# A block of ripple attention and mixture of experts: adding DMAs merge weighted terms that TensorE summed alone, and identity turns stand ahead of three more of its waits

## The chip, the cores and the metric

The kernel runs on one core of a Trainium2 chip. The metric is the time of one execution on the device in microseconds (us); the time before is the median of three runs. A core has TensorE (PE in the profile; its weight loads are PEld), VectorE (DVE), ScalarE (ACT), GpSimd (POOL) and SyncE (SP), each with its own queue of instructions that it works off in order, and 16 DMA engines that carry the transfers of all queues. Engines wait for each other by semaphores. TensorE's granted clock is given as a share of 2.4 GHz: 1.00 or, at the lower level of 1.2 GHz, 0.50.

## What is computed

The input x has four batches of 1024 tokens with 128 channels, in float32. The block is x + LN(attention(LN(x))), called x2, and then x2 + LN(experts(LN(x2))). The attention is a sum of three parts:

```
offsets = 0, 1, 2, 4, ..., 512                      # 11 earlier positions of each token
tele = softmax(q . k[pos - offsets] / 4) weighs v[pos - offsets]     # 8 heads of 16 channels
conv = 7 taps along the tokens, per channel, of v
low  = elu features of q and k: fq (fk^T v) / (fq . sum fk)
attention = x + (tele + conv + low) @ Wo
```

The feed-forward part sends each token to two of eight experts by a sigmoid gate, each a hidden layer of 64 with GELU, and adds a shared expert. All of it must come out; the change touches how the 11 weighted terms of `tele` and the term `low` are added up, and in what order that happens.

## The kernel before

The four batches run through a pipeline. In iteration b of the main loop (b = 0 to 4) the attention of batch b runs beside the experts of batch b - 1, which are cut into two halves of 512 tokens, called units: u0 = 2b - 2 and u1 = 2b - 1. Also beside it run the layer norm and the projections of batch b + 1. There is no planner: the order on each engine is written out by hand in five program blocks (SyncE, POOL, ScalarE, VectorE, TensorE), and each waits on semaphores with the counts that the other blocks raise.

A batch has eight tiles of 128 tokens. In the stage that the change touches, VectorE weighs the values of tile j (`weigh`, L929 to L950; its instructions are L940): three multiplications write up to 11 terms of 128 x 128 into one of four buffers in SBUF (TERM_BUFS = 4), first those with whole-tile offsets, then the offset 128, then in one instruction the seven shifted ones (1 to 64), 128 x 896 elements. Between them it works off steps of the gates of u1, for tiles 0 to 3 and only where there are experts to do (b > 0). TensorE then sums the terms of the tile (`sum_terms`, L1252 to L1265): a turn against the identity for the low-rank term (L1260) and one for each live term (L1263), all accumulated in one PSUM bank, so that the sum arrives turned. Tiles 0 to 3 fill the bank as the first half of the batch, tiles 4 to 7 as the second. When a half is there, VectorE adds the convolution to it (`add_conv`, L967 to L972), which frees the bank, and TensorE takes the output product (`output`, L1267 to L1275):

```
live = [m for m in range(NV) if TERMS[m] < P or TERMS[m] // P <= j]
for m in live:
    ins = pe.matmul(dst, terms[:, j % TERM_BUFS, m, :], ident[:], is_transpose=True,
                    start=False, stop=(m == live[-1]))
```

The order of the terms in a buffer is 128, 512, 256, 0, 1, 2, 4, 8, 16, 32, 64. Tile 0 has 8 live terms, tile 4 and those behind it 11.

Around these sums TensorE's queue also holds the experts: the sum over the experts of u0 (`experts_out`, L1358) in front of tile 0, the projections of q and v of batch b + 1 (`project`, L1183) in front of tiles 1 and 5, hidden layers of u1 (L1322) in front of tile 2, the turn of the gates of u1 (L1332) in front of tile 4 and its spread gates (`spread_gates`, L1344) in front of tiles 5 and 6. VectorE needs the spread gates for `gate_hidden` (L1063), which stands in its queue behind tiles 5 and 7. In front of all this come, for u1, the turn of x3 (`turn_x3`, L1284), the gate logits (`gate_logits`, L1295), and the turned logits (`turn_logits`, L1301); for u0 they come earlier in the iteration, between the sums of the scores (L1231).

POOL's queue in an iteration holds the 1/sqrt steps of the layer norms (`rstd_of`, L433 and L435), the tap sums of the convolution as DMAs that add (`add_tap`, L453 and L454, 512 KB each), and for the experts the scale of u0's outputs (`ln4`, L489), and the addition of the residual (`add_residual`, L497 to L502, line L501), which waits for ScalarE's `scale_outputs` (L700). The part that matters is, in this order: the last tap sums, `ln4(u0)`, `add_residual(u0)`, `ln2(2b)`, then the first tap sums of the next batch. SyncE's queue stores the outputs of u0 when `add_residual` is done, and behind that loads the x of batch b + 2 (L338).

`keep_busy(n, bank)` (L1363 to L1367) runs n turns of the identity into a PSUM bank, whose results nobody reads; before the change it stands at the kernel's start, ahead of the last score sums (12 turns) and at three places in the tail.

Of the kernel before, what the change touches and what calls it, by code (L numbers as in the profile page):

```python
# [20 lines left out]
P = 128  # L21
# [27 lines left out]
WARM_UP = 28  # L49
FILL_SUM = 12  # L50
FILL_FRONT = 5
CH = 5


N_DMA = 16
SHIFT_ROWS = 112
N_SHIFT_DMA = 16 * sum(3 if P - off > SHIFT_ROWS else 2 for off in SHIFTS)
N_PSA_FULL, N_PSA_FREE = 16, 14
# [14 lines left out]
LAST_BANKS = (0, 1, 2, 3, 0, 1, 2, 0)  # L73

LAST_GATE_STEPS = (12, 15, 18, 21)


def upto(b, per_batch, n):
# [37 lines left out]
def block_kernel(nc, x, Wqkv, Wo, conv_w, gate_W, W1, b1, W2, b2, Ws1, bs1, Ws2, bs2, route_scale, out):  # L116
# [4 lines left out]
    with ExitStack() as ctx:  # L121
# [6 lines left out]
        def sem(name):  # L128
            return ctx.enter_context(nc.semaphore(name))
# [109 lines left out]
        logit_ready, prob_ready, softmax_step = sem("logit_ready"), sem("prob_ready"), sem("softmax_step")  # L239
        v_shifted, low_ready, low_used = sem("v_shifted"), sem("low_ready"), sem("low_used")  # L240
        terms_ready, terms_summed = sem("terms_ready"), sem("terms_summed")
        tap_scaled, sums_added, side_added = sem("tap_scaled"), sem("sums_added"), sem("side_added")
        conv_step = sem("conv_step")
        hT_ready, y_ready = sem("hT_ready"), sem("y_ready")
# [134 lines left out]
        def _(pool):  # L379
# [64 lines left out]
            def ln1(b):  # L444
# [5 lines left out]
                pool.wait_ge(ln1_step, upto(b - 1, 2, 2))  # L450
                nc.gpsimd.tensor_tensor(nmr1[:], neg_mean[:, b % 3, :], rstd1[:], ALU.mult).then_inc(ln1_ready, 1)

            def add_tap(b, into, tap, added):  # L453
                nc.gpsimd.dma_start(tap_home(b, into), tap_home(b, tap), accum_op=ALU.add).then_inc(added, N_DMA)  # L454

# [51 lines left out]
            for b in range(B + 1):  # L507
                attn, ffn, more = b < B, b >= 1, b < B - 1
                u0, u1 = 2 * b - 2, 2 * b - 1
                if ffn:  # L510
                    ln2(u1)
                if 2 <= b < B:
                    ln4(u0 - 1)
                if attn and b:
                    sum_taps_second(b)
                if more:
                    ln1(b + 1)
                if ffn and attn:
                    ln3(u1)
                if attn and b:  # L520
                    sum_taps_third(b)
                if ffn and attn:
                    ln4(u0)
                    add_residual(u0)
                if attn:
                    ln2(2 * b)
                if more:
                    sum_taps_first(b + 1)
                if attn:
                    ln3(2 * b)  # L530
                if not attn:
                    ln3(u1)
                    ln4(u0 - 1)
                    ln4(u0)
                    ln4(u1)
# [265 lines left out]
        def _(dve):  # L801
# [278 lines left out]
            for b in range(B + 1):  # L1080
# [29 lines left out]
                if attn:  # L1110
# [14 lines left out]
                    for j in range(NT):  # L1125
                        def two_gate_steps(n):

                            if ffn and j < TPH:
                                gates(u1, range(2 * (3 * j + n), 2 * (3 * j + n + 1)))

                        weigh(b, j, two_gate_steps)
                        if ffn:
                            if j in (5, 7):
                                gate_hidden(u1, range(j - 5, j - 3))
                        if j == TPH:
                            add_conv(b, 0)
                    residual(2 * b)
                    add_conv(b, 1)
                    if more:
# [16 lines left out]
        def _(pe):  # L1156
# [95 lines left out]
            def sum_terms(b, j):  # L1252

                pe.wait_ge(terms_ready, upto(b, NT, j + 1))
                if j == 0:
                    pe.wait_ge(low_used, b + 1)
                elif j == TPH:
                    pe.wait_ge(hT_ready, upto(b, 2, 1))
                dst = psH[:, bass.ts(j % TPH, P)]
                pe.matmul(dst, low_terms[:, j, :], ident[:], is_transpose=True, start=True, stop=False)  # L1260
                live = [m for m in range(NV) if TERMS[m] < P or TERMS[m] // P <= j]
                for m in live:
                    ins = pe.matmul(dst, terms[:, j % TERM_BUFS, m, :], ident[:], is_transpose=True,  # L1263
                                    start=False, stop=(m == live[-1]))
                ins.then_inc(terms_summed, 1)  # L1265
# [18 lines left out]
            def turn_x3(u):  # L1284

                if u == 2 * B - 1:
                    pe.wait_ge(front_free, upto(u, N_FRONT, 0))
                elif u:
                    pe.wait_ge(hidden_free, upto(u, N_HIDDEN, -1))
                pe.wait_ge(xn3_ready, u + 1)  # L1290
                for n, j in enumerate(unit_tiles(u)):
                    ins = pe.transpose(front(u, X3)[:, bass.ts(n, P)], xn3[:, j, :], ident[:])
                ins.then_inc(front_full, 1)

            def gate_logits(u):  # L1295
                if 0 < u < 2 * B - 1:
                    pe.wait_ge(hidden_free, upto(u, N_HIDDEN, 0))
                pe.wait_ge(front_free, upto(u, N_FRONT, 1))
                pe.matmul(front(u, C4), w1[:, 4 * P:5 * P], x3T[:, half_cols(u)], start=True, stop=True).then_inc(front_full, 1)

            def turn_logits(u):  # L1301
                pe.wait_ge(front_free, upto(u, N_FRONT, 2))
                for n, j in enumerate(unit_tiles(u)):
                    ins = pe.transpose(front(u, LOGITS)[:, bass.ts(n, EXPERTS)], gate_shared[0:EXPERTS, bass.ts(j, P)],
# [193 lines left out]
```

## Time and profile before

| what | us |
|---|---|
| median of three runs (302.92 to 304.26) | 303.39 |
| the profiled execution, its own time | 304.41 |
| its span in the profile | 302.7 |
| TensorE busy in the span | 248.6 (82%) |
| VectorE busy | 240.0 (79%) |
| ScalarE busy | 192.6 (64%) |
| POOL busy | 84.4 (28%) |

The rows below come from the one profiled execution. Times of day in it are us from the start of its span; some 1.7 us of its own time lie outside the span. A busy share is a mean over stages that have different limits, so it doesn't say which engine a stage waits for. That is read from the timeline: an instruction's row ends, in brackets, with the idle time of its engine just before it and the instruction that ended this idle time. Durations of neighbouring instructions overlap a little, since the engines are pipelined.

### The profile page before, as it was taken

How to read it: one execution, taken by the hardware profiler on the slowest of the kernel's cores; microseconds unless marked ns; L12 is line 12 of the kernel's file. 1: busy time of each engine (PE TensorE's matmuls, PEld its weight loads, DVE VectorE, ACT ScalarE, POOL GpSimd, SP SyncE). 2: the span in 40 equal slices, each digit the busy share in tenths (PEclk: the TensorE clock that was granted, in tenths of full speed). 3: DMA queues.
4: the chain of work that ended last, by engine and by line, in shares of the span. 5: the costliest groups of instructions: out<-in, count | busy, mean ns of one | idle time of the engine just before them, and what ended most of it. 6: DMA issues, size and time to landing. Idle time of an engine off the chain costs nothing.

```text
span 302.7 us, 4600 instructions
## 1 busy us (share of the span) xinstructions
PE 248.6 (82%) x1559; PEld 170.7 (56%) x1559; DVE 240.0 (79%) x573; ACT 192.6 (64%) x458; POOL 84.4 (28%) x145
## 2 busy tenths in 40 slices
PE   5756875788499879998888799989897897699893
PEld 5334351777164538777644367778454586584383
DVE  6299989976986699679988699599967997817743
ACT  1681067227849964798788845898698334375851
POOL 4923000004307011222764103025641131230013
PEclk9989599599979979999999989999999799999999
DMA  7406831001979930304999820108899701000003
GB/s 212 112 0 177 250 88 34 0 2 27 226 226 219 198 73 0 96 10 77 239 241 218 182 45 0 37 0 163 240 234 212 153 0 35 2 0 2 2 5 99
DMA packets 22945, 31.32 MB, mean 103 GB/s; under 512 B 3893, under 2 KB 17038, under 8 KB 22922
## 3 DMA queue, kind: packets, MB, share of 16 engines
q1 hardware_dynamic: 20330, 21.59, 24.7%
q0 software_dynamic: 2592, 9.44, 17.8%
q8 instruction: 12, 0.20, 0.3%
q14 instruction: 11, 0.09, 0.1%
HBM read 5.07 MB, written 2.10 MB: 24 GB/s over the span
## 4 chain that ended last, share of the span: by engine, by line
PE 42%; ACT 26%; DVE 21%; POOL 5%; issue 4%; DMA 1%; POOLq 0%; DVEq 0%; ACTq 0%
PE psH L1263 7%; PE psA L1183 5%; PE psF L1322 5%; PE psY L1358 4%; DVE prods L940 4%; ACT xn L645 3%; PE psA L1231 3%; ACT xn L555 3%; DVE prods L269 3%; PE psA L1358 3%; ACT squares L638 3%; POOL rstd L435 2%; PE psY L1212 2%; PE psA L1175 2%; POOL var L433 2%
## 5 line engine op out<-in xcount | busy, mean ns | idle before, releaser
L269 DVE TENSOR_TENSOR prods<-qT,kT 128x1024 f32<-128x1024 f32 (+1 forms) x44 | 49.3, 1176 | 3.8 <-ACT qT L541 3.8
L433 POOL TENSOR_SCALAR var<-ss 128x4 f32<-128x4 f32 (+1 forms) x25 | 11.7, 470 | 137.6 <-ACT squares L631 64.9
L1263 PE MATMUL psH<-ident,prods 128*128 128x128 f32 x324 | 42.8, 284 | 0.0
L1263 PEld LDWEIGHTS psH<-ident,prods 128*128 128x128 f32 x324 | 39.1, 148 | 2.3 <-issue 2.3
L940 DVE TENSOR_TENSOR prods<-v_shift,prob 128x896 f32<-128x896 f32 x32 | 34.7, 1083 | 0.0
L1063 DVE TENSOR_TENSOR hid<-hid,psG 128x512 f32<-128x512 f32 x32 | 20.8, 683 | 16.0 <-PE psG L1344 15.4
L435 POOL TENSOR_TENSOR rstd<-var,neg_half 128x4 f32<-128x4 f32 (+2 forms) x28 | 32.3, 1155 | 2.3
L1322 PE MATMUL psF<-x3T,w 128*128 128x512 f32 x58 | 31.0, 646 | 0.4 <-ACT gexp L659 0.3
L1231 PE MATMUL psA<-prods,slot_sel 128*32 128x512 f32 x168 | 24.7, 636 | 6.9 <-DVE prods L269 5.6
L1183 PE MATMUL psA<-xnT,wqkv 128*128 128x512 f32 x48 | 26.2, 683 | 3.3 <-ACT xnT L541 3.3
L940 DVE TENSOR_TENSOR prods<-v_tok,prob 128x128 f32<-128x128 f32 (+2 forms) x60 | 20.7, 372 | 0.0
L667 ACT ACTIVATE hid<-psF,b1c 128x512 f32<-128x512 f32 x29 | 18.8, 685 | 2.7 <-PE psF L1322 2.5
L454 POOL DMA_DIRECT2D convT<-tapT x9 | 8.2, 913 | 43.3 <-DMA convT<-tapT 26.0
L1322 PEld LDWEIGHTS psF<-x3T,w 128*128 128x128 f32 x58 | 10.7, 207 | 14.3 <-issue 11.4
L1358 PEld LDWEIGHTS psY<-w,hid 128*128 128x128 f32 x140 | 16.1, 192 | 3.6 <-DVE prods L924 2.6
L1260 PE MATMUL psH<-ident,prods 128*128 128x128 f32 x32 | 9.6, 300 | 9.8 <-DVE prods L940 5.8
L1358 PE MATMUL psY<-w,hid 128*128 128x128 f32 x140 | 16.4, 276 | 1.2 <-DVE prods L924 1.2
L555 ACT ACTIVATE xn<-x_in,nmr,rstd 128x128 f32<-128x128 f32 x32 | 12.9, 484 | 6.4 <-DVE nmr L826 5.3
L1183 PEld LDWEIGHTS psA<-xnT,wqkv 128*128 128x128 f32 x48 | 8.5, 203 | 13.7 <-ACT xnT L541 4.8
L1231 PEld LDWEIGHTS psA<-prods,slot_sel 128*32 128x32 f32 x168 | 5.2, 112 | 16.4 <-issue 8.5
L1367 PEld LDWEIGHTS psG<-ident 128*128 128x128 f32 x76 | 10.8, 168 | 6.3 <-issue 3.2
L1367 PE MATMUL psG<-ident 128*128 128x128 f32 x76 | 11.5, 317 | 3.1 <-POOL ident L389 3.1
(213 smaller groups left out, 561.6 us busy)
## 6 DMA issues: line engine op xcount, KB each, us to landing
v_shift<-v_tok SPq DMA_DIRECT2D x20, 448.0 KB
convT<-tapT POOLq DMA_DIRECT2D x9, 512.0 KB, 5.1
x_in<-L_attn_x SPq DMA_DIRECT2D x4, 512.0 KB, 3.7
x_res<-L_attn_x SPq DMA_DIRECT2D x4, 512.0 KB, 10.3
out<-y_out SPq DMA_DIRECT2D x7, 256.0 KB, 2.3
v_shift<-v_tok SPq DMA_DIRECT2D x4, 384.0 KB
tapT<-tapT POOLq DMA_DIRECT2D x3, 512.0 KB, 9.2
convT<-kexp POOLq DMA_DIRECT2D x3, 512.0 KB, 7.6
```

What stands on the lines that cost most here:

```text
L269: return eng.tensor_tensor(prods[:, QUADS * (s % 2) + q, t0:T], qT[:, t0:T], kT[:, PRE - off + t0:PRE - off + T], ALU.mult)
L435: return nc.gpsimd.tensor_tensor(rstd[:, cols], var[:, cols], neg_half[:, cols], ALU.pow)
L555: nc.scalar.activation(xn[:, j, :], x_in[:, j, :], ACT.Identity, bias=nmr1[:, j:j + 1], scale=rstd1[:, j:j + 1]).then_inc(xn_ready, 1)
L667: nc.scalar.activation(hid[:, c, half_cols(u)], hidden_bank(u, c), ACT.Gelu, bias=b1c[:, c:c + 1]).then_inc(hidden_free, 1)
L940: return nc.vector.tensor_tensor(dst, src.rearrange("p m (h d) -> p m h d", d=HD), w, ALU.mult)
L1063: nc.vector.tensor_tensor(hid[:, c, cols], hid[:, c, cols], psG[:, c % 2, :], ALU.mult).then_inc(gated, 1)
L1183: pe.matmul(psA[:, half, :], wqkv[:, bass.ts(part, P)], xnT[(b + 1) % 2][:, bass.ts(half, HALF)], start=True, stop=True).then_inc(psA_full, 1)
L1231: ins = pe.matmul(psA[32 * q:32 * q + 32, half, :], ksum_sel[:] if low else slot_sel[:, s, :], fqT[:, cols] if low else prods[:, QUADS * ( ...
L1263: ins = pe.matmul(dst, terms[:, j % TERM_BUFS, m, :], ident[:], is_transpose=True, start=False, stop=(m == live[-1]))
L1322: pe.matmul(hidden_bank(u, c), w1[:, bass.ts(c, P)], x3T[:, half_cols(u)], start=True, stop=True).then_inc(hidden_full, 1)
L1358: ins = pe.matmul(output_tile(u, n), hid[:, c, bass.ts(j, P)], w2[:, c, :], start=(c == CH - 1), stop=(c == CH - 2))
L1367: pe.transpose(bank[:, bass.ts(k % TPH, P)], ident[:], ident[:])
```

## The change

Four edits. First, for tiles 0 to 5 of batches 0 to 2 and tiles 0 to 3 of batch 3, POOL issues a DMA that adds a block of terms of the tile onto another block in the same buffer: for tiles 0 to 3 the three terms of offsets 1, 2 and 4 onto those of 8, 16 and 32, for tiles 4 and 5 the five terms of offsets 128, 512, 256, 0 and 1 onto those of 2, 4, 8, 16 and 32. TensorE waits for that DMA behind the turn of the low-rank term, and leaves the merged blocks out: three turns fewer for tiles 0 to 3, five fewer for tiles 4 and 5. POOL issues the merges of tiles 0 to 2 behind its last tap sums, that of tile 3 behind `ln4(u0)`, and those of tiles 4 and 5 behind `add_residual(u0)`. Second, VectorE adds the convolution to the first half behind the weighing of tile 5, and no longer behind that of tile 4. Third, TensorE runs ten identity turns ahead of its wait for x3 of the even units 2 and 4. Fourth, it runs four ahead of the gate logits and eight ahead of the turned logits of the odd units 1, 3 and 5.

```diff
+FILL_X3, FILL_C4, FILL_LOGITS = 10, 4, 8
+MERGE_TILES = 6
+def merged_terms(b, last, j):
+    if j >= (TPH if b == last else MERGE_TILES):
+        return 0, 0, 0
+    return (0, 5, 5) if j >= TPH else (M_SHIFT, M_SHIFT + 3, M_SHIFT + 3)
...
+            def merge_terms(b, tiles):
+                for j in tiles:
+                    m0, m1, into = merged_terms(b, B - 1, j)
+                    if m1:
+                        pool.wait_ge(terms_ready, upto(b, NT, j + 1))
+                        buf = terms[:, j % TERM_BUFS]
+                        nc.gpsimd.dma_start(buf[:, into:into + m1 - m0, :], buf[:, m0:m1, :],
+                                            accum_op=ALU.add).then_inc(terms_merged[j % TERM_BUFS], N_DMA)
...
                 if attn and b:
                     sum_taps_third(b)
+                if attn:
+                    merge_terms(b, range(0, 3))
                 if ffn and attn:
                     ln4(u0)
+                if attn:
+                    merge_terms(b, range(3, 4))
+                if ffn and attn:
                     add_residual(u0)
                 if attn:
+                    merge_terms(b, range(4, NT))
                     ln2(2 * b)
...
                         weigh(b, j, two_gate_steps)
+                        if j == TPH + 1:
+                            add_conv(b, 0)
                         if ffn:
                             if j in (5, 7):
                                 gate_hidden(u1, range(j - 5, j - 3))
-                        if j == TPH:
-                            add_conv(b, 0)
...
                 pe.matmul(dst, low_terms[:, j, :], ident[:], is_transpose=True, start=True, stop=False)
-                live = [m for m in range(NV) if TERMS[m] < P or TERMS[m] // P <= j]
+                m0, m1, into = merged_terms(b, B - 1, j)
+                if m1:
+                    before = sum(merged_terms(a, B - 1, i)[1] > 0 for a in range(b) for i in range(j % TERM_BUFS, NT, TERM_BUFS))
+                    pe.wait_ge(terms_merged[j % TERM_BUFS], N_DMA * (before + 1 + j // TERM_BUFS))
+                live = [m for m in range(NV) if (TERMS[m] < P or TERMS[m] // P <= j) and not m0 <= m < m1]
...
+                if 0 < u < 2 * B - 2 and u % 2 == 0:
+                    keep_busy(FILL_X3, front(u, X3))
                 pe.wait_ge(xn3_ready, u + 1)
...
+                if u < 2 * B - 2 and u % 2:
+                    keep_busy(FILL_C4, front(u, C4))
                 pe.wait_ge(front_free, upto(u, N_FRONT, 1))
...
+                if u < 2 * B - 2 and u % 2:
+                    keep_busy(FILL_LOGITS, front(u, LOGITS))
                 pe.wait_ge(front_free, upto(u, N_FRONT, 2))
```

## Rows read from the trace of the kernel before

**Rows 1.** The page's chain that ended last: shares of the span by engine

```profile
PE 42%; ACT 26%; DVE 21%; POOL 5%; issue 4%; DMA 1%; POOLq 0%; DVEq 0%; ACTq 0%
```

**Rows 2.** The chain in order of time, batch 1: start, us, what

```profile
108.27 3.46 PE psA L1183 x4
...
113.67 4.46 PE psY L1358 x40
```

**Rows 3.** Windows: busy time by engine, granted clock (PEclk), DMA share, GB/s

```profile
56.00:60.00 4.00, 4.00 (x20) 4.00 (x19) 4.00 (x10) 0.00 (x0) 0.00 (x0) 0.50 0.00 0
60.00:64.00 4.00, 3.12 (x25) 2.92 (x24) 2.45 (x5) 0.00 (x0) 0.00 (x0) 0.89 0.00 0
...
110.00:111.00 1.00, 1.00 (x3) 0.48 (x2) 0.93 (x3) 0.60 (x1) 0.00 (x0) 0.50 1.05 197
128.00:128.50 0.50, 0.50 (x7) 0.50 (x6) 0.45 (x1) 0.50 (x1) 0.00 (x0) 1.00 1.09 329
```

**Rows 4.** Timeline of batch 1: start, us, engine, line, operation, idle before

```profile
107.09 0.41 PE L1304 MATMUL psF<-ident,gate_shared 8*128 8x8 f32 x4 [0.92 <-ACT gate_shared L541]
...
111.53 0.68 DVE L924 TENSOR_TENSOR prods<-psY,prob 128x512 f32<-128x512 f32 x1
...
118.19 1.08 DVE L940 TENSOR_TENSOR prods<-v_shift,prob 128x896 f32<-128x896 f32 x1
...
119.69 1.08 POOL L435 TENSOR_TENSOR rstd<-var,neg_half 128x4 f32<-128x4 f32 x1
...
120.61 1.08 DVE L940 TENSOR_TENSOR prods<-v_shift,prob 128x896 f32<-128x896 f32 x1
...
121.37 1.14 ACT L700 ACTIVATE y_out<-psY,rstd 128x128 f32<-128x128 f32 x4
...
122.59 1.08 DVE L940 TENSOR_TENSOR prods<-v_shift,prob 128x896 f32<-128x896 f32 x1
...
122.65 2.17 POOL L501 TENSOR_TENSOR y_out<-y_out,x 128x512 f32<-128x512 f32 x1 [1.88 <-ACT y_out L700]
...
126.09 0.69 DVE L972 TENSOR_TENSOR prods<-psH,convT 128x512 f32<-128x512 f32 x1 [2.41 <-PE psH L1263]
...
127.06 1.36 PE L1263 MATMUL psH<-ident,prods 128*128 128x128 f32 x11
...
130.11 1.28 DVE L1063 TENSOR_TENSOR hid<-hid,psG 128x512 f32<-128x512 f32 x2 [1.67 <-PE psG L1344]
```

**Rows 5.** Timeline of batch 1, POOL's step ahead of the residual

```profile
134.88 1.02 POOL L435 TENSOR_TENSOR rstd<-var,neg_half 128x4 f32<-128x4 f32 x1
```

**Rows 6.** The page's costliest groups: POOL's issue of an adding DMA

```profile
L454 POOL DMA_DIRECT2D convT<-tapT x9 | 8.2, 913 | 43.3 <-DMA convT<-tapT 26.0
```

**Rows 7.** DMA issues: an adding DMA at 107.34 us, and one at 162.28 us

```profile
convT<-tapT POOLq DMA_DIRECT2D x1, 512.0 KB, 4.5
...
convT<-tapT POOLq DMA_DIRECT2D x1, 512.0 KB, 9.3
```

**Rows 8.** Timeline of batch 2: the turn of x3, and identity turns

```profile
147.96 0.66 PE L1292 MATMUL psF<-ident,xn 128*128 128x128 f32 x4
...
148.65 0.60 ACT L541 ACTIVATE x3T<-psF 128x512 f32<-128x512 f32 x1
...
156.22 1.47 PE L1367 MATMUL psG<-ident 128*128 128x128 f32 x12
```

**Rows 9.** Timeline of batch 3, VectorE and POOL

```profile
249.41 1.28 POOL L501 TENSOR_TENSOR y_out<-y_out,x 128x512 f32<-128x512 f32 x1 [1.38 <-ACT y_out L700]
...
252.31 0.68 DVE L972 TENSOR_TENSOR prods<-psH,convT 128x512 f32<-128x512 f32 x1
...
256.32 1.28 DVE L1063 TENSOR_TENSOR hid<-hid,psG 128x512 f32<-128x512 f32 x2 [1.66 <-PE psG L1344]
```

**Rows 10.** Timeline of batch 0, VectorE

```profile
59.85 1.08 DVE L940 TENSOR_TENSOR prods<-v_shift,prob 128x896 f32<-128x896 f32 x1
...
62.48 0.69 DVE L972 TENSOR_TENSOR prods<-psH,convT 128x512 f32<-128x512 f32 x1 [1.55 <-PE psH L1263]
```

More of the change, by code:

```diff
@@ L241, in block_kernel @@
         terms_ready, terms_summed = sem("terms_ready"), sem("terms_summed")
+        terms_merged = [sem(f"terms_merged{i}") for i in range(TERM_BUFS)]
         tap_scaled, sums_added, side_added = sem("tap_scaled"), sem("sums_added"), sem("side_added")
```

## The prediction

> **What bounds the kernel now.** I read the shares of the chain that ended last first [rows 1]: TensorE holds 42% of it, ScalarE 26%, VectorE 21%. No engine bounds alone, so each edit must be priced in its own stage. The chain in order of time [rows 2] leads through the stage that the change touches, in batch 1 as 65 us later in batch 2: four projections at 108.27 that take 3.46 us, then the expert sums at 113.67. The windows [rows 3] show why they are slow: the granted clock is 0.50, the lower level of 1.2 GHz, after TensorE had sat through waits such as the 0.92 us before 107.09 [rows 4]. Next I read the timeline of batch 1 [rows 4] for the sums of the eight tiles. VectorE weighs without a stop and finishes the terms of tile 2 at 119.27, of tile 3 at 121.69, of tile 4 at 123.67; it then idles 2.41 us until the sum of tile 3 is out (126.09) and 1.67 us more until the spread gates come (130.11). From 130.11 on it doesn't pause. It reaches the end of its stage at about 136.0, when POOL's 1/sqrt for the next residual ends too, 135.90 [rows 5]. So two paths arrive together, and a gain needs both earlier; a loss needs only one later.
>
> **The change, part by part.** The sum goes against the profiled execution: 304.41 us, span 302.7, so 1.7 us lie around it; it stands 1.02 us above the median of the runs, 303.39.
>
> *What an adding DMA costs.* POOL spends 0.91 us to issue one [rows 6]. The tap sum of 512 KB lands 4.5 us after its issue on idle DMA engines and 9.3 us beside other transfers [rows 7]. Its data move at 197 GB/s [rows 3], so 2.7 of the 4.5 us are data and 1.8 are fixed. Three terms (192 KB) then land after 1.8 + 1.0 = 2.8 us, five (320 KB) after 1.8 + 1.7 = 3.5 us, the latter at most 3.5 + 4.8 x 320/512 = 6.5 us. The page "DMA: Bandwidth & Descriptors" of the Trainium skill (Anatomy of one DMA) fits 2.0 us + bytes/436 GB/s instead. That would be 3.2 us for the 512 KB, where the row has 4.5, so this trace disagrees; by it the sum below would be about 1.5 us smaller, 309 us.
>
> *Batches 1 and 2, tiles 0 to 3.* Each sum loses three turns; twelve turns take about 1.4 us (1.36 for eleven [rows 4]), 0.11 each, so 0.33 a tile. Tiles 0 to 2 land by the time TensorE comes. For tile 3, POOL's order decides: it waits for tile 2's terms (119.27) and issues (0.91), and only then comes the 1/sqrt for the outputs, which ran at 119.69 before; it now ends near 121.7 instead of 120.77. Tile 3's merge is issued at about 121.8, lands at 124.6, and its seven turns end at 125.4 instead of 126.0: 0.6 us earlier for what ScalarE does next.
>
> *Tile 4, the step that decides.* Ahead of its merge POOL's queue holds the addition of the residual (122.65, 2.17 us). This waits for the scaled outputs, 1.14 us of ScalarE from 121.37 on [rows 4], now until about 122.9. It takes 1.28 us at the least [rows 9] and 2.17 when VectorE is busy; VectorE now weighs tile 5 there instead of idling, so I take 2.17. The merge is issued at 125.1 (124.2 at the earliest) and lands 3.5 us later, at 128.6. In batch 1 the load of the next x and the output's store use the DMA engines just then (329 GB/s at 128 us [rows 3]); I take 0.9 us more, 129.5. Batch 2 has no load there: 0.3 more, 128.9. Bounds: 127.7 and, with the 6.5 us, 131.6. TensorE waits for it in front of tile 4's remaining turns (0.7 us), and behind that wait stand in its queue the output product, the spread gates and the projection of v. Before, the sum ended at 128.42 and VectorE got its gates at 130.11, 1.69 later. Now it gets them at landing + 0.7 + 1.7. Even is a landing at 127.7. So batch 1 loses 1.8 us, batch 2 1.2 us, each between 0 and 3.9. A gain is excluded, because 127.7 is also the earliest. VectorE's pause simply moves; tile 5's weighing, put ahead of the convolution's addition, uses up its first part without letting the gates come sooner. Tile 5's merge has long landed when its sum is due: the projection of v lies between. Behind POOL's merges stand the 1/sqrt of the half-batch and the tap sums, due some 8 us later [rows 5]: nothing.
>
> *Turns before the logits.* Four before the gate logits and eight before the turned logits; eight are 0.9 us, against a wait of 0.92 [rows 4]. That wait hides them; uncovered, they would cost up to 1.3 us a batch. If they hold 2.4 GHz, the projections cost 1.7 us less [rows 2], of which 1.3 are usable, as the expert sums can't start before 112.2 (the second low-rank product, 111.53 + 0.68 [rows 4]). TensorE then stands earlier in front of terms that VectorE and the merges set: 0.
>
> *Ten turns before the turn of x3, batches 2 and 3.* Twelve such turns take 1.47 us [rows 8], ten 1.2. In batch 2 the turn runs at 147.96, directly behind the score sums, and ScalarE takes its result at 148.65, 0.03 us after its end: nothing to hide behind. I take 0.9 us a batch, bounds 0 (POOL may be the last link later) and 1.2.
>
> *Batch 3.* Here VectorE is the late one: the convolution's addition follows tile 4's terms at 252.31 without a wait, and tile 5's weighing then ends at 256.32 - 1.66 = 254.66 [rows 9], 1.7 us after it. Put ahead, it moves the addition, tile 4's sum and the gates by 1.7 us. At most 1.2 come back if POOL's 1.28 us, which lay across VectorE's work at 249.41, fall into a pause. I take 1.5, bounds 0.5 and 1.7.
>
> *Batch 0.* TensorE is at 1.2 GHz and VectorE waits 1.55 us for the sum of tile 3 [rows 10]. Its tile 3 terms are done at about 59.2, one weighing (1.7) before tile 4's at 60.93; the merge lands at 62.1, seven turns at half clock take 1.5: 63.6 against 62.4. The shorter sums of tiles 4 and 5 give some back: +0.7, bounds 0 and 2.
>
> Sum: 0.7 + 1.8 + 1.2 + 2 x 0.9 + 1.5 = +7.0, so 311.4 for a profiled execution and **310.4** as the median. The bounds alone give 304 to 316.
>
> **Rivals.** *The clock carries it (faster).* The turns hold 2.4 GHz at 108 and 173 us, TensorE comes 1.3 us earlier, and tile 4's merge lands by 126.4, in time for a sum that follows the convolution's addition at once; then VectorE's gates come 1.35 us earlier in both batches and the x3 turns fall into new waits: 303.4 - 2.7 + 0.5 = 301 us. The landing decides: 127.7 is even. For it speaks how near TensorE's own path lies; against it, that the merge can't be issued before 124.2. The windows [rows 3] do show that turns raise the clock: from 56 us on TensorE does nothing but turns, first at 0.50, then at 0.89 between 60 and 64. "TensorE: Matmul & The Clock Gate" of the Trainium skill (Part 4) says that a transpose does not count as work for the full clock. By it these turns would give back nothing and this rival would fall; the trace disagrees.
>
> *Everything at its lower end (no change).* POOL gets its addition through in 1.28 us, the transfers don't meet, the x3 turns hide: about 303.9.
>
> *The clock falls in the new waits (slower still).* In front of tile 4 TensorE now waits some 3 us; if it drops to 0.50 as at 110 us, four projections and three sums cost 1.7 us more in each of batches 0 to 2: 315.
>
> **The numbers.** Forecast 0.48 (306 to 313.5), faster rival 0.20, no change 0.18, clock falls 0.14. The range 300.5 to 314.5 leaves out half of the last case and some of the faster one. A measurement tells 0.5%, 1.5 us, from no change: faster 0.20, same 0.17 (most of the third), slower 0.63.
>
> **What would show it.** Right: in batch 1 TensorE idles some 3 us behind the low-rank turn of tile 4, released by a DMA; VectorE's wait for its gates grows by 1 to 3 us; POOL's addition ends after 124.5; ScalarE takes x3 about 1 us later in batches 2 and 3; the addition in batch 3 follows tile 5. The granted clock is 1.00 at 108 to 112. Wrong: a merge of five terms that lands by 126.5, or gates before 130.

## The result, and the profile after

The changed kernel takes **319.12 us** (median of 4 runs, 318.98 to 319.28); the kernel before takes 303.66 us beside it. The ratio is 1.0504, 95% interval 1.0466 to 1.0542: 15.5 us slower, where the forecast was 7.0 and its range ended at 314.5. The profiled execution took 319.02 us, its span is 317.3 us. Where one run of a kernel below lies over 1.5% above its fastest, the median of the others follows in square brackets.

The page of the changed kernel, the chain that ended last by engine, and two of the costliest groups (busy us, mean ns | idle before, releaser). The first line answers to [rows 1]:

```profile
PE 39%; DVE 28%; ACT 16%; POOL 7%; DMA 6%; issue 4%; POOLq 0%; DVEq 0%; ACTq 0%
...
L1293 PE MATMUL psH<-ident,prods 128*128 128x128 f32 x246 | 37.9, 304 | 16.5 <-DMA prods<-prods 16.5
...
L470 POOL DMA_DIRECT2D prods<-prods x22 | 19.2, 874 | 62.6 <-DVE prods L966 62.6
```

Transfers, 1% of the chain before, now hold 6% of it, TensorE's turns of terms wait 16.5 us for merges, and POOL spends 19.2 us on issuing 22 of them. To find where, I follow two instructions of VectorE through each batch: the masked product of the linear state (kv), and the convolution's addition for tiles 4 to 7. For batch 1 of the changed kernel the timeline has them here:

```profile
92.95 0.28 DVE L914 TENSOR_TENSOR kv<-psY,head_mask 128x128 f32<-128x128 f32 x1
...
142.90 0.68 DVE L998 TENSOR_TENSOR prods<-psH,convT 128x512 f32<-128x512 f32 x1
```

This stretch, 142.90 - 92.95 = 49.95 us, is called the stage below. From one batch's second addition to the next kv it takes 21.3 us ahead of batch 2 and 17.3 ahead of batch 3 in every kernel of this study. Ahead of batch 1 this lead-in takes 18.7 to 21.4 us; two profiles of the kernel before had 20.2 with a stage of 45.0, and 18.7 with 45.9. So stage 1 is compared safely only at equal lead-ins. Each figure is the difference of two such rows; "batch 0" is the time at which its second addition starts.

| kernel | time, us | batch 0 | lead-in 1 | stage 1 | stage 2 | stage 3 |
|---|---|---|---|---|---|---|
| before | 303.7 | 71.8 | 20.2 | 45.0 | 43.8 | 43.6 |
| changed | 319.1 | 72.8 | 20.1 | 50.0 | 47.5 | 48.0 |
| turns ahead of the logits alone | 301.0 | 69.5 | 21.3 | 43.8 | 42.6 | 43.6 |
| x3 turns alone | 305.8 | 71.8 | 20.2 | 45.0 | 44.0 | 45.0 |
| moved addition alone | 307.1 | 72.7 | 21.4 | 45.3 | 43.9 | 45.3 |
| turns ahead of the logits + addition | 307.7 | 72.1 | 18.7 | 46.6 | 43.9 | 46.9 |
| all but the merges | 309.4 | 71.0 | 18.7 | 46.5 | 44.2 | 47.7 |
| merges alone | 316.7 | 73.5 | 18.7 | 49.6 | 47.2 | 46.2 |
| changed, POOL's merges first | 317.3 | 72.9 | 20.1 | 47.6 | 46.7 | 45.9 |

The loss of the changed kernel lies in the stages: 1.0 us in batch 0, then 4.9, 3.7 and 4.4, and 0.7 after the last addition, 14.7 us in all against 14.6 between the spans. The timeline of batch 1 shows how, beside [rows 4]:

```profile
109.21 1.98 PE L1209 MATMUL psA<-xnT,wqkv 128*128 128x512 f32 x4 [0.77 <-ACT xnT L567]
...
113.13 3.06 PE L1394 MATMUL psY<-w,hid 128*128 128x128 f32 x25 [0.23 <-DVE prods L950]
...
121.61 1.85 POOL L445 TENSOR_TENSOR rstd<-var,neg_half 128x4 f32<-128x4 f32 x1
...
123.43 0.91 POOL L470 DMA_DIRECT2D prods<-prods  x1
...
124.47 1.82 DVE L966 TENSOR_TENSOR prods<-v_tok,prob 128x384 f32<-128x384 f32 x2
...
124.80 1.34 POOL L521 TENSOR_TENSOR y_out<-y_out,x 128x512 f32<-128x512 f32 x1 [0.45 <-ACT y_out L726]
...
126.09 0.87 POOL L470 DMA_DIRECT2D prods<-prods  x1
...
126.54 0.98 PE L1293 MATMUL psH<-ident,prods 128*128 128x128 f32 x7 [2.01 <-DMA prods<-prods]
...
127.56 0.69 DVE L998 TENSOR_TENSOR prods<-psH,convT 128x512 f32<-128x512 f32 x1 [0.27 <-PE psH L1293]
...
131.48 1.54 PE L1293 MATMUL psH<-ident,prods 128*128 128x128 f32 x6 [2.79 <-DMA prods<-prods]
...
135.52 0.78 PE L1380 MATMUL psG<-gT,gate_sel 24*128 24x512 bf16 x2
...
136.12 1.28 DVE L1089 TENSOR_TENSOR hid<-hid,psG 128x512 f32<-128x512 f32 x2 [7.87 <-PE psG L1380]
```

The four projections take 1.98 us instead of 3.46. Then POOL's queue runs as forecast: 1/sqrt, merge of tile 3, residual, merge of tile 4 (issued at 126.09; 125.1 was forecast, and 0.93 us of the difference comes from batch 0, since kv stands at 92.95 where it stood at 92.02). TensorE waits 2.01 us for tile 3's merge and 2.79 for tile 4's. VectorE gets its gates at 136.12 after 7.87 us without work; before, at 130.11 after 1.67. The windows of this stretch add what the timeline doesn't say (busy by engine, granted clock, DMA share, GB/s; they answer to [rows 3]):

```profile
110.00:111.00 1.00, 1.00 (x3) 0.38 (x2) 0.97 (x2) 0.60 (x1) 0.00 (x0) 1.00 1.06 205
...
129.00:130.00 1.00, 0.00 (x0) 0.00 (x0) 0.00 (x0) 0.98 (x2) 0.00 (x0) 0.54 1.12 143
...
132.00:133.00 1.00, 1.00 (x6) 1.00 (x5) 0.00 (x0) 1.00 (x2) 0.00 (x0) 0.50 1.18 248
```

At 110 us the clock is 1.00 where it was 0.50; at 132 it is 0.50 where TensorE had been at 1.00. So six turns that take 0.88 us at full clock (below, with POOL's merges first) take 1.54, and the output product runs from 132.82 to 135.5 at 1.2 GHz. From its issue at 126.09 tile 4's merge takes 5.35 us to land (chain in order of time, then the list of DMA issues from 123 to 134 us; its last column is us from issue to landing, the median where there are two):

```profile
126.09 5.35 DMA prods<-prods
```

```profile
prods<-prods POOLq DMA_DIRECT2D x2, 320.0 KB, 6.0
...
x_in<-L_attn_x SPq DMA_DIRECT2D x1, 512.0 KB, 6.2
out<-y_out SPq DMA_DIRECT2D x1, 256.0 KB, 2.4
```

Both five-term merges, the store that the residual releases and the next load are under way together. Which of them delays the landing is taken up at the end.

### The profile page after: what moved, and what is told of

It is laid out like the page before. It is cut to its first block, busy times and chain, and to the rows that moved or that the text cites. A ratio compares the mean times of both kernels' runs of the same rounds, so it can differ in the third digit from the quotient of the medians.

```text
span 317.3 us, 4573 instructions
## 1 busy us (share of the span) xinstructions
PE 250.4 (79%) x1537; PEld 170.8 (54%) x1537; DVE 242.0 (76%) x573; ACT 193.0 (61%) x458; POOL 101.9 (32%) x167
## 4 chain that ended last, share of the span: by engine, by line
PE 39%; DVE 28%; ACT 16%; POOL 7%; DMA 6%; issue 4%; POOLq 0%; DVEq 0%; ACTq 0%
DVE prods L966 6%; PE psH L1293 5%; DMA prods<-prods 5%; PE psA L1257 4%; POOL rstd L445 4%; DVE hid L1089 3%; ACT xn L581 3%; PE psG L1394 3%; DVE prods L279 3%; PE psA L1394 3%; PE psA L1201 3%; PE psF L1333 2%; PE psF L1358 2%; ACT xn L671 2%; PE psY L1238 2%
## 5 line engine op out<-in xcount | busy, mean ns | idle before, releaser
L1293 PE MATMUL psH<-ident,prods 128*128 128x128 f32 x246 | 37.9, 304 | 16.5 <-DMA prods<-prods 16.5
L1293 PEld LDWEIGHTS psH<-ident,prods 128*128 128x128 f32 x246 | 31.6, 157 | 21.4 <-DMA prods<-prods 20.5
L470 POOL DMA_DIRECT2D prods<-prods x22 | 19.2, 874 | 62.6 <-DVE prods L966 62.6
L445 POOL TENSOR_TENSOR rstd<-var,neg_half 128x4 f32<-128x4 f32 (+2 forms) x28 | 35.7, 1276 | 2.3
L443 POOL TENSOR_SCALAR var<-ss 128x4 f32<-128x4 f32 (+1 forms) x25 | 10.3, 411 | 75.1 <-ACT squares L657 29.5
L1358 PE MATMUL psF<-x3T,w 128*128 128x512 f32 x58 | 29.0, 610 | 0.4 <-ACT gexp L685 0.3
L1209 PE MATMUL psA<-xnT,wqkv 128*128 128x512 f32 x48 | 23.1, 611 | 3.3 <-ACT xnT L567 3.3
L966 DVE TENSOR_TENSOR prods<-v_tok,prob 128x128 f32<-128x128 f32 (+2 forms) x60 | 23.9, 424 | 0.5 <-PE psH L1293 0.5
L1286 PE MATMUL psH<-ident,prods 128*128 128x128 f32 x32 | 10.0, 313 | 8.2 <-DVE prods L966 5.8
L1358 PEld LDWEIGHTS psF<-x3T,w 128*128 128x128 f32 x58 | 9.7, 189 | 12.5 <-issue 8.5
L657 ACT ACTIVATE squares<-psY 128x128 f32<-128x128 f32 x16 | 4.2, 275 | 18.2 <-PE psY L1304 18.2
```

What stands on the lines that cost most here:

```text
L445: return nc.gpsimd.tensor_tensor(rstd[:, cols], var[:, cols], neg_half[:, cols], ALU.pow)
L470: nc.gpsimd.dma_start(buf[:, into:into + m1 - m0, :], buf[:, m0:m1, :], accum_op=ALU.add).then_inc(terms_merged[j % TERM_BUFS], N_DMA)
L966: return nc.vector.tensor_tensor(dst, src.rearrange("p m (h d) -> p m h d", d=HD), w, ALU.mult)
L1209: pe.matmul(psA[:, half, :], wqkv[:, bass.ts(part, P)], xnT[(b + 1) % 2][:, bass.ts(half, HALF)], start=True, stop=True).then_inc(psA_full, 1)
L1358: pe.matmul(hidden_bank(u, c), w1[:, bass.ts(c, P)], x3T[:, half_cols(u)], start=True, stop=True).then_inc(hidden_full, 1)
```

## Experiments

**Turns ahead of the logits alone.** The kernel before plus that part, written as edits of the changed kernel:

```
-FILL_X3, FILL_C4, FILL_LOGITS = 10, 4, 8
+FILL_X3, FILL_C4, FILL_LOGITS = 0, 4, 8
 merged_terms: every tile returns 0, 0, 0
 add_conv(b, 0) back behind the terms of tile 4
```

> The kernel before with the identity turns ahead of the gate logits and the turned logits, and nothing else of the change. Theory (the prediction's term 0): the turns lie in waits, the four projections fall from 3.46 to about 2 us, and TensorE then stands earlier in front of terms that VectorE sets: 303.2 to 304.2 us. Rival (the full clock that they hold is worth what the projections lose, 1.3 us a batch in batches 1 and 2): 301 us.

301.03 us, ratio 0.9902 (0.9866 to 0.9939): the rival's number, not mine. The timeline of batch 1:

```profile
107.09 1.98 PE L1209 MATMUL psA<-xnT,wqkv 128*128 128x512 f32 x4 [0.78 <-ACT xnT L567]
...
123.70 0.69 DVE L998 TENSOR_TENSOR prods<-psH,convT 128x512 f32<-128x512 f32 x1 [0.20 <-PE psH L1293]
```

The first addition now waits 0.20 us for tile 3's sum instead of the 2.41 of [rows 4]. TensorE was the late one there, so what it gains counts: stages 1 and 2 shrink by 1.2 us each, though in batch 1 a longer lead-in takes it back in this profile, and batch 0, whose instructions are the same, ends 2.3 us earlier. So of the 3.6 us between the two spans 2.3 lie in batch 0. The granted clock is 1.00 from 108 to 112 us. By Part 4 of "TensorE: Matmul & The Clock Gate" of the Trainium skill, transposes don't count as work for the full clock; the rows disagree, with 1.00 at 110 us behind the turns and 0.50 in [rows 3] without them.

**Two second profiles.** The kernel before, and the changed kernel, once more.

> The kernel before once more, for a second profile. Theory (the gain of the kernel with the turns ahead of the logits alone came in batch 2 and, by the clock, in batch 0 by chance): batch 0 ends again at 71.8 us at one clock and at 69.5 at another, and batches 1 and 2 take the 65.2 and 65.1 us of the first profile. Rival (the gain in batch 0 belongs to the other program): 71.8 us again.

303.95 us. Batch 0 ends at 71.89 us again, as the rival said; the stages are 45.9, 43.8 and 43.6. One more profile of this kernel doesn't settle whether the 2.3 us of batch 0 came by chance in the run above; what differs there is the granted clock from 56 to 58 us, 0.50 before and 0.76 with the turns.

> The changed kernel once more, for a second profile. Theory: the stages of the tile sums repeat within 0.3 us (49.9, 47.5 and 48.0 us from the first product of the linear state to the second addition in batches 1 to 3), and what differs lies in batch 0 and the start of batch 1. Rival (the half clock behind the waits comes and goes): one of the three shorter by 1.5 us or more.

318.91 us; batch 0 at 72.8, stages of 49.90, 47.54 and 47.99. The half clock behind the waits is no accident of one run.

**Merges alone.** All three FILL constants 0, the addition at its old place.

> The kernel before with the merges alone: no turns, the addition at its old place. Prediction's steps: 0.7 in batch 0, 1.8 and 1.2 in batches 1 and 2, none in batch 3: 307.2 us. Theory of now (the merge of tile 4 lands 4.3 to 5.3 us after its issue and half clock follows the wait): about 1 in batch 0, 4.5 to 5 and 3.5 in batches 1 and 2, up to 0.5 in batch 3: 312.5 to 314 us. Rival (the merges hurt only because the turns bring TensorE to them earlier): 308 us or less.

316.74 us [316.06], ratio 1.0431 (1.0381 to 1.0481). The merges make most of the loss by themselves, and without the turns: 1.7 us in batch 0, 3.1 in batch 1 (4.5 in its stage, after a lead-in 1.4 shorter), 3.4 and 2.6 in stages 2 and 3. The chain in order of time has tile 4's merges of batches 1 and 2 in it, each from its issue to its landing; the timeline has the issue of tile 5's merge of batch 1, 4.2 us behind tile 4's:

```profile
125.53 5.32 DMA prods<-prods
...
195.05 4.18 DMA prods<-prods
```

```profile
129.73 0.85 POOL L470 DMA_DIRECT2D prods<-prods  x1 [3.34 <-DVE prods L966]
```

I had given batch 3 at most 0.5 us. There no merge of tile 4 exists, but the addition waits 2.98 us for the sum of tile 3, whose merge POOL issues behind its 1/sqrt at 258.91 (timeline of batch 3; before, [rows 9], it had no wait):

```profile
257.08 1.85 POOL L445 TENSOR_TENSOR rstd<-var,neg_half 128x4 f32<-128x4 f32 x1
258.91 0.91 POOL L470 DMA_DIRECT2D prods<-prods  x1
...
263.00 0.69 DVE L998 TENSOR_TENSOR prods<-psH,convT 128x512 f32<-128x512 f32 x1 [2.98 <-PE psH L1293]
```

**No merges of tiles 4 and 5**, and **no merges at all**: MERGE_TILES = 4 in the one, merged_terms returning zeros in the other, all else as changed.

> The changed kernel without the five-term merges of tiles 4 and 5. Theory (the merge of tile 4 lands behind POOL's addition of the residual, and TensorE cools down in front of it): most of the 4.9 and 3.7 us of batches 1 and 2 come back, and what is left is batch 0 with 1.0, the x3 turns with 1.1, batch 3 with 3.5 and about 1 us of the wait for tile 3: about 310 us (308 to 312). Rival (the three-term merges of tiles 0 to 3 and the moved addition carry the loss): 316 to 318 us.

313.12 us [311.76], ratio 1.0266 (1.02 to 1.0331), at the upper end of the theory's range; its runs spread from 310.5 to 315.9.

> The changed kernel without any merge: the turns and the moved addition alone. Theory (the merges carry the loss of batches 0 to 2, and the turns ahead of the logits gain 2.4 us): 301.0 + 0.3 + 0.8 for the x3 turns + 1.6 for the addition in batch 3 = 303.7 us (302.5 to 306). Rival (the moved addition delays the gates by about 1.5 us in each of batches 1 to 3): 307 us. Prediction's terms: 303.4 + 1.8 + 1.5 = 306.7 us.

309.35 us, ratio 1.0206 (1.0152 to 1.026). Against 319.1, the five-term merges of tiles 4 and 5 cost some 6 to 7 us and the three-term ones some 2 to 4, 9.8 us together. Even without a merge the changed kernel is 8.3 us slower than with the turns ahead of the logits alone, above every number that I had put down. The next runs divide these 8.3 us: 307.70 without the x3 turns too, so 1.65 for them, and the other 6.7 for the moved addition beside the turns ahead of the logits.

**The moved addition**, alone, and beside the turns ahead of the logits.

```
                         weigh(b, j, two_gate_steps)
+                        if j == TPH + 1:
+                            add_conv(b, 0)
...
-                        if j == TPH:
-                            add_conv(b, 0)
```

> The kernel before with the convolution's addition moved behind the terms of tile 5, and nothing else of the change. Prediction's step: nothing in batches 1 and 2, where VectorE pauses 2.4 us for the sum of tile 3 anyway, 1.5 us in batch 3: 305.2 us (304.3 to 305.6). Theory of now: the same in batches 1 and 2, since TensorE is late there without the turns, and in batch 3 1.7 us plus about 1.6 for the half clock behind the longer wait: 306.5 us. Rival (it costs 1.5 us or more in each batch): 308 us.

307.11 us, ratio 1.0105 (1.0037 to 1.0172). Stages 1 and 2 grow by 0.3 and 0.1 us, stage 3 by 1.7: the prediction's step at its upper bound (it took 1.5), without the half clock that I had added. Batch 0 loses 0.8 us, and the lead-in of batch 1 is among the long ones.

> The kernel before with the turns ahead of the logits and the moved addition, without merges and without the x3 turns. Theory (with the turns, TensorE has tile 3's sum ready when VectorE ends tile 4's terms, so VectorE's pause is 0.2 us instead of 2.4 and tile 5's weighing delays the addition by 1.5 us in each of batches 1 to 3, and half clock follows where TensorE waits for it): from the first product of the linear state to the second addition, batches 1 and 2 take about 46.5 and 44 us (43.8 and 42.6 with the turns alone), batch 3 45.3 to 47 us; 305 to 308 us. Rival (the price of the move is that of batch 3 alone, 1.7 us, and the rest is the x3 turns'): 302.5 us.

307.70 us, ratio 1.0137 (1.009 to 1.0184): the theory's numbers in all three stages (46.6, 43.9, 46.9). Timeline of batch 1, then one window:

```profile
122.23 1.25 PE L1293 MATMUL psH<-ident,prods 128*128 128x128 f32 x10
...
124.92 0.68 DVE L998 TENSOR_TENSOR prods<-psH,convT 128x512 f32<-128x512 f32 x1
...
125.74 0.30 PE L1286 MATMUL psH<-ident,prods 128*128 128x128 f32 x1 [1.93 <-DVE prods L998]
125.88 2.46 PE L1293 MATMUL psH<-ident,prods 128*128 128x128 f32 x11
...
130.58 1.28 DVE L1089 TENSOR_TENSOR hid<-hid,psG 128x512 f32<-128x512 f32 x2 [4.99 <-PE psG L1380]
```

```profile
126.00:128.00 2.00, 2.00 (x12) 2.00 (x11) 0.00 (x0) 1.99 (x3) 0.00 (x0) 0.50 0.04 8
```

The sum of tile 3 is out at 123.5. VectorE is weighing tile 5 and adds only at 124.92; TensorE waits 1.93 us, falls to 1.2 GHz, and its eleven turns take 2.46 us instead of the 1.36 of [rows 4]. From the end of that sum to the second addition it takes 13.9 us here and 11.0 with the turns alone: the turns had removed the pause that made the move free.

**The x3 turns**, alone on the kernel before, and left out of the changed kernel (FILL_X3 = 10 alone; FILL_X3 = 0).

> The kernel before with the ten turns ahead of the turn of x3 alone. Prediction's step: 0.9 us each in batches 2 and 3: 305.4 us. By the trace of the changed kernel (0.3 and 0.8): 304.7 us. Rival (the clock that they hold pays for them): 303.6 us or less.

305.84 us, ratio 1.0054 (1.0026 to 1.0082): +0.2 us in stage 2 and +1.4 in stage 3, 1.6 against the 1.8 of the forecast, though not where it put them.

> The changed kernel without the ten turns ahead of the turn of x3. By the prediction (0.9 us each in batches 2 and 3): 317.3 us. By the trace of the changed kernel (0.3 in batch 2, 0.8 in batch 3): 318.0 us. Rival (they were hidden, and hold the clock): 319 us or more.

316.81 us, ratio 1.0404 (1.0336 to 1.0472). Stage 3 is 45.6 instead of 48.0: 0.8 us are gained up to the first addition, and 1.6 behind it by the clock, which is 1.00 in the 6 us from that addition on, where the changed kernel has 0.68 and 0.75. That leaving out the x3 turns is what holds the clock isn't shown: the kernel with the turns ahead of the logits and the moved addition has no x3 turns either, and there it falls (12.4 us from the first addition to the second, 10.9 here).

**The addition put back** in the changed kernel.

> The changed kernel with the convolution's addition put back behind the terms of tile 4. Theory (it costs in batch 3 alone, where VectorE is the late one; in batches 1 and 2 the merge of tile 4 ends last anyway): 1.5 us less, 317.6 us. Rival (the addition sets the sum of tile 4 in every batch, so that the move costs about 1.5 us in each of three): 314.6 us. Second rival (the wait for tile 3's sum comes back into VectorE's queue and delays tile 5): no gain, 319 us.

317.68 us [317.41], ratio 1.0421 (1.0364 to 1.0479): the theory's number, but in batch 3 by another path, which is luck. In the profile stage 3 gets 1.6 us back (46.4 against 48.0), stage 2 gets 0.2, and stage 1 0.5 after a lead-in 1.4 shorter; in batches 1 and 2 the merge of tile 4 ends last. In batch 3 the addition comes no earlier than in the changed kernel, 35.53 us after kv in both, since at its old place it waits for the late sum of tile 3. What comes back is the clock behind it (timelines of batch 3, first the changed kernel, then this one):

```profile
264.56 0.69 DVE L998 TENSOR_TENSOR prods<-psH,convT 128x512 f32<-128x512 f32 x1 [0.23 <-PE psH L1293]
...
265.54 2.46 PE L1293 MATMUL psH<-ident,prods 128*128 128x128 f32 x11
```

```profile
262.79 0.69 DVE L998 TENSOR_TENSOR prods<-psH,convT 128x512 f32<-128x512 f32 x1 [2.95 <-PE psH L1293]
...
263.76 1.36 PE L1293 MATMUL psH<-ident,prods 128*128 128x128 f32 x11
```

In front of tile 3's merged terms TensorE waits 1.98 us in the changed kernel and 0.28 here.

**POOL's merges first.**

```
-                    merge_terms(b, range(0, 3))
+                    merge_terms(b, range(0, 5))
 (ln4: the 1/sqrt of the outputs)
-                    merge_terms(b, range(3, 4))
+                    merge_terms(b, range(5, NT))
 (add_residual)
-                    merge_terms(b, range(4, NT))
```

> The changed kernel, with POOL's order changed: the merges of tiles 3 and 4 ahead of the 1/sqrt of the outputs, the merge of tile 5 behind it and ahead of the addition of the residual. Theory (POOL's order makes the merges of tiles 3 and 4 late): in batch 1 tile 4's merge is issued at 124.6 us instead of 126.1 and lands 1.5 us or more earlier, and so do the gates, in batches 1 and 2, and tile 3's sum comes 0.8 us earlier in batch 3: 315 to 317 us. Rival (the transfers themselves are slow, or ScalarE, whose scaling of the outputs now comes later, takes the place of the landing): 318.5 to 320 us.

317.25 us [316.75], ratio 1.0472 (1.0395 to 1.0549); the runs spread over 6.5 us, so the time alone tells no gain. The profile does (batch 1; lines are one lower than in the changed kernel): first the timeline, then the DMA issues from 123 to 134 us, then the chain.

```profile
124.97 0.85 POOL L470 DMA_DIRECT2D prods<-prods  x1 [1.15 <-DVE prods L965]
...
128.61 0.88 PE L1292 MATMUL psH<-ident,prods 128*128 128x128 f32 x6 [0.44 <-DMA prods<-prods]
...
131.67 1.28 DVE L1088 TENSOR_TENSOR hid<-hid,psG 128x512 f32<-128x512 f32 x2 [3.95 <-PE psG L1379]
```

```profile
prods<-prods POOLq DMA_DIRECT2D x2, 320.0 KB, 3.6
```

```profile
126.48 1.04 POOL rstd L445
...
127.54 1.14 ACT y_out L725 x4
...
131.87 1.28 ACT L623
133.17 1.06 ACT kexp L623
```

With 2.5 us between the two five-term merges and the store behind them, each lands 3.6 us after its issue. TensorE waits 0.44 us, keeps its clock, and the gates come 4.45 us earlier, at 131.67. But stage 1 shrinks by 2.4 only, because ScalarE scales the outputs 4.0 us later (127.54 against 123.50), and the chain then runs through its exponentials. Both theories hold in part: the order makes the merges late, and what is put behind them is late next.

**The clock held.** Identity turns into a free bank ahead of TensorE's waits for the merges of tiles 3 and 4, and for the addition.

```
+                    if b:
+                        keep_busy(6, psG[:, 0, :])
                     pe.wait_ge(hT_ready, upto(b, 2, 1))
...
+                if b and j in (3, 4) and m1:
+                    keep_busy(16 if j == 3 else (None, 22, 12)[b], psG[:, 0, :])
                 if m1:
...
                     pe.wait_ge(terms_merged[j % TERM_BUFS], ...)
```

> The changed kernel, with identity turns into a free bank ahead of the waits of TensorE for the merges of tiles 3 and 4 and for the addition that tile 4's sum follows (16, 22 or 12, and 6 of them, in batches 1 to 3). No wait is taken away; TensorE only stays busy in them. Theory (half clock behind the waits costs some 2 us in each of three batches, on top of the late merge): 313 to 315 us, with a granted clock of 1.00 in the output product of batch 1 that ran at 0.50. Rival (the landing of the merge alone costs, and the clock nothing, since POOL's residual and VectorE come later anyway): 317.5 to 320 us.

315.07 us [314.87], ratio 1.037 (1.0327 to 1.0413), within the theory's range. The brackets leave out 388.1 us; the profile is of one more run of the same kernel:

> The changed kernel with identity turns in the waits for the merges once more, for its profile. Theory: the granted clock is 1.00 in tile 4's turns, the output product and the spread gates of batches 1 to 3; from the addition of one batch's second half to the next, batches 1 to 3 take about 68, 67 and 63.5 us instead of 70.1, 68.8 and 65.3. Rival: the same spans as the changed kernel, at a higher clock.

317.99 us, less of a gain than in the timed runs. The clock is 1.00 in all three stages, but from one batch's second addition to the next it takes 69.1, 68.9 and 64.4 us, not the theory's 68, 67 and 63.5. In batch 1 (timeline) the clock gives 2.1 us between landing and gates, though the lead-in is 1.2 longer:

```profile
131.80 0.88 PE L1297 MATMUL psH<-ident,prods 128*128 128x128 f32 x6 [0.25 <-DMA prods<-prods]
...
134.36 1.28 DVE L1089 TENSOR_TENSOR hid<-hid,psG 128x512 f32<-128x512 f32 x2 [5.72 <-PE psG L1384]
```

From 131.80 to 134.36 are 2.56 us, against 131.48 to 136.12, 4.64, in the changed kernel. In batch 2 nothing is left of it, because there the merge of tile 4 takes longer (chain in order of time, then DMA queues and issues from 193 to 203 us):

```profile
194.62 6.03 DMA prods<-prods
```

```profile
q8 instruction: 1, 0.02, 1.1%
...
prods<-prods POOLq DMA_DIRECT2D x2, 320.0 KB, 6.1
out<-y_out SPq DMA_DIRECT2D x1, 256.0 KB, 2.3
```

The changed kernel had 4.5 there. Why the same two merges and the same store took 1.6 us more is open. The list has one thing that the changed kernel's lacks in this stretch, the packet of 0.02 MB on a queue for instructions; whether it delays the merges isn't shown.

**A faster version.** The turns ahead of the logits alone, and 40 more in batch 0's longest wait.

```
+                    if b == 0:
+                        keep_busy(40, psG[:, 1, :])
                     for j in range(NT):
```

> The kernel with the turns ahead of the logits alone, and 40 more identity turns in batch 0, in the 4.9 us for which TensorE waits for the first terms. Theory (what batch 0 takes is set by TensorE's clock: it sums tiles 0 to 3 at half clock): the clock is 1.00 from 54 to 62 us, the addition of the first half starts at 60 us whatever the run, and the median falls from 301.0 to 299 to 300.5 us. Rival (VectorE's terms set the end of batch 0): 301 us, as without them.

299.87 us, ratio 0.9859 (0.9811 to 0.9908), the best of the study and faster than both kernels. The first addition of batch 0 starts at 59.95 us, against 62.48 in [rows 10] and 60.18 without the 40 turns. Whether the 40 turns add anything to the other twelve isn't settled: 297.5 to 301.6 against 299.5 to 301.9 us.

## Why the prediction was right in sign and less than half in size

The forecast was 7.0 us; measured were 15.5, outside the range. Three steps failed: the landing of tile 4's merge was taken too short, full clock was taken for granted behind TensorE's wait for it, and batch 3 has no term for tile 3's late merge and for the half clock. One sum is off as well: the bounds of the parts add up to 304 to 317, not 316.

**Tile 4, batches 1 and 2: mechanism right, two terms short.** The queue behind POOL's residual, the issue at 125.1 (126.09 less 0.93 is 125.2) and the wait for a DMA came as written. Mis-sized was the landing, "3.5 us later" plus 0.9 and 0.3 for traffic: it took 5.35 and 4.3. The 3.5 itself is right, 3.6 for tile 4's merge in batch 0 and with POOL's merges first, where no store or load runs beside it; the traffic cost about 1.7 and 0.7. It was not the merge of tile 5: with the merges alone that one was issued 4.2 and 4.1 us behind, and tile 4's took 5.32 and 4.18 all the same. What the slow landings have in common is the store, and in batch 1 the load; no run takes them away. And "landing + 0.7 + 1.7" assumed full clock: it was 4.64 and 4.2 us. So batch 1 lost 1.8 + 0.95 (5.35 - 4.4) + 2.2 = 4.95, measured 4.9; batch 2 lost 1.2 + 0.5 + 1.8 = 3.5, measured 3.7, about 0.2 of it by the x3 turns if they cost there what they cost alone. A second path is close in batch 2: the chain of the changed kernel goes through tile 3's merge (3.04 us from 193.71) and POOL's next 1/sqrt, and without the x3 turns through tile 4's (4.26 from 196.21).

**The clock rival was not a rival.** The prediction gave it 0.14, as a case instead of the forecast. It is a consequence of the same wait and belonged into the sum: in batches 1 and 2 the stage pays the wait and the half clock behind it. With the prediction's own price of 1.7 us for batches 1 and 2, the sum would have been 313.8. Holding the clock showed it, 2.1 us in batch 1.

**Tile 3 and batch 3: two terms at nothing.** "Lands at 124.6, and its seven turns end at 125.4 instead of 126.0: 0.6 us earlier" was worked out for batches 1 and 2. POOL's 1/sqrt ahead of that merge took 1.85 us, not the 1.08 of [rows 4], and in batch 1 the sum came 0.5 us later than before (the addition at 127.56, less 0.93, against 126.09). For batch 3 the sum has no term for it. There VectorE doesn't wait for that sum before, so three fewer turns gain nothing and a late merge costs everything: 2.6 us by the merges alone. In the changed kernel this cost and that of the moved addition overlap: the first addition starts 35.5 us after kv with the addition at either place, 35.2 without merges, and 32.9 before. So up to there batch 3 loses 2.7 us, near the 2.4 forecast (1.5 and 0.9), though the 1.5 now stands for two causes at once. The other 1.7 us of its 4.4 lie behind that addition: eleven turns at half clock, 2.46 us instead of 1.36, and half of the output product.

**The turns ahead of the logits: 0 was wrong.** By themselves they shorten stages 1 and 2 by 1.2 us each, and the run by 2.85; in the profile 2.3 of 3.6 us lie in batch 0. The argument that TensorE "stands earlier in front of terms that VectorE and the merges set" overlooked the 2.41 us in [rows 4], in which VectorE waits for TensorE. In the changed kernel the merge of tile 4 ends last in batches 1 and 2, so the forecast's net seems to come out right for the wrong reason; no run takes these turns out of the changed kernel. The faster rival had the size, 1.35 us a batch, and tied it to a landing that never came.

**The moved addition: right alone, wrong in company.** 1.7 us in batch 3 and next to nothing in batches 1 and 2 hold for the kernel before. With the turns, VectorE's pause is gone, and the move costs 2.9 us in batch 1 (13.9 against 11.0, above), 1.3 in batch 2 (43.9 against 42.6) and 3.3 in batch 3 (46.9 against 43.6, half of it the clock). Edits were priced one by one against the trace of before, and two of them spend the same pause.

**x3 and batch 0.** 1.8 forecast, 1.6 measured, split 0.2 and 1.4 instead of evenly; in batch 2 POOL is the last link (the chain with these turns alone goes through its steps from 157.11 to 160.36), the reason given for the lower bound. Batch 0: 0.7 forecast, 1.0 measured. The 0.7 us after the last addition was not foreseen; its cause is open.

## What to carry to other kernels

A wait that you add to TensorE can have two prices, the time until the data land and the clock behind it; put both into one sum. Price a new transfer beside the transfers that start in the same moment, here the store that the residual ahead of the merge releases, and the load behind it. And where one edit closes a pause in which another edit was free, price them together.

## What was unexpected in the hardware

An adding DMA of 320 KB landed 3.6 us after its issue in batch 0, with tile 5's merge 1.7 us behind it and no store or load beside it. Beside the store of 256 KB (batch 2) tile 4's took 4.2 to 4.3, and beside the store and the load of 512 KB (batch 1) 5.3, whether tile 5's merge followed after 1.5 us or after 4.1 to 4.2. No run takes the store or the load away. The 6.03 us in batch 2 of the held clock are the exception. Three-term merges of 192 KB landed in 2.9 to 3.3 in the changed kernel.

POOL's 1/sqrt of 128 x 4 took 1.85 us where VectorE had just begun a product of 896 elements (121.48; the 1/sqrt at 121.61, above), and 1.01 to 1.08 in most other places. VectorE's pair of products took 1.82 us beside POOL's addition (124.47, above), and 0.75 without it. "SBUF — State Buffer" of the Trainium skill (SBUF: two separate sides) says that a VectorE instruction with two inputs in SBUF and a GpSimd instruction that reads SBUF exclude each other from a pair of ports for the whole instruction. The trace agrees as far as these durations go, but not throughout: VectorE's pair at 122.80 took its usual 0.75 us inside that 1/sqrt.

After waits of nearly the same length the clock fell at different moments. In the changed kernel the 2.79 us ahead of tile 4 in batch 1 came after 2.01 us ahead of tile 3; the clock was at 0.54 from 129 to 130 us already, and six turns took 1.54 us. With the merges alone, 2.68 us came after 0.68, and six turns from 130.89 on took 0.97; the clock fell behind them, as windows of that kernel show:

```profile
131.00:132.00 1.00, 1.00 (x8) 1.00 (x9) 0.00 (x0) 1.00 (x3) 0.00 (x0) 0.76 1.24 316
132.00:133.00 1.00, 1.00 (x7) 1.00 (x7) 0.00 (x0) 1.00 (x2) 0.00 (x0) 0.50 1.06 202
```

What decides isn't settled by these runs.
